# SiLU once instead of twice, its rounded part by a copy, and new orders around it, in a three-pass attention block

## The reference

```python
win = x cut into 8x8 windows                     # 16 windows of 64 tokens in an image
q, k, v = split(layernorm(win, ln1) @ in_w.T + in_b)          # 8 heads of 16
attn = softmax(q @ k.T / 4)                      # in a window
y = win + (attn @ v) @ out_w.T + out_b
h = layernorm(y, ln2)
y = y + silu(h @ fc1_w.T + fc1_b) @ fc2_w.T + fc2_b           # hidden width 256
# second layer, over the 1024 tokens of an image
q, k, v = wq @ y + bq, wk @ y + bk, wv @ y + bv               # width 64
out = wo @ ((q @ k.T / N) @ v) + bo + y
```

## Time and profile before

| | us |
|---|---|
| median of 3 runs | 342.38 (340.73 to 343.91) |
| the profiled execution, run time | 343.58 |
| its span in the profile | 341.8 |
| one even step (start of `b_score` to the next) | 17.39 |
| one odd step | 20.77 |
| epilogue, from its `b_score` to the end | 44.37 |

### The profile page before, as it was taken

How to read it: one execution, slowest core, us unless ns; L and a number is a source line. 1 busy time by engine, 2 the same in 40 slices (tenths; PEclk the granted TensorE clock), 3 DMA queues, 4 the chain that set the end, 5 groups by cost and what they waited for, 6 DMA issues and landing times. The chain is left out here.

```text
span 341.8 us, 9704 instructions
## 1 busy us (share of the span) xinstructions
PE 319.7 (94%) x3424; PEld 268.4 (79%) x3424; DVE 273.9 (80%) x851; ACT 238.4 (70%) x446; POOL 165.6 (48%) x177
## 2 busy tenths in 40 slices
PE   6789898999999999999999999999999999999675
PEld 5678787888787888778887888788887888787554
DVE  4776788988798969888798969898798879686752
ACT  5555486877869596967869595977878695955260
POOL 6514555538265544538265554537264653422430
PEclk9989899999999999999999999999999999999895
DMA  4442021221504032221404042222404041210011
GB/s 138 110 103 49 3 71 54 58 72 42 144 12 109 10 96 91 48 79 47 141 15 101 13 106 82 65 64 55 132 17 105 13 107 44 71 24 2 0 64 61
DMA packets 31888, 22.36 MB, mean 65 GB/s; under 512 B 22433, under 2 KB 23777, under 8 KB 31841
## 3 DMA queue, kind: packets, MB, share of 16 engines
q1 hardware_dynamic: 31744, 21.62, 23.3%
q10 hardware_dynamic: 96, 0.13, 0.1%
HBM read 4.95 MB, written 4.19 MB: 27 GB/s over the span
## 5 line engine op out<-in xcount | busy, mean ns | idle before, releaser
L1213 ACT ACTIVATE probs<-p_scoreT 128x512 f32<-128x512 f32 x64 | 37.8, 591 | 45.6 <-PE p_scoreT L781 44.8
L542 POOL TENSOR_TENSOR hid_l<-hid,hid_h 128x512 fp32r<-128x512 f32 x30 | 40.0, 1345 | 46.4 <-ACT hid_h L1248 40.4
L1504 DVE TENSOR_REDUCE row_max<-p_x 128x8 f32<-128x512 f32 x64 | 43.2, 683 | 7.7 <-PE p_x L749 7.7
L796 PEld LDWEIGHTS p_attn<-vd,probs 128*64 128x64 f32 x1024 | 36.2, 140 | 14.2 <-issue 9.5
L796 PE MATMUL p_attn<-vd,probs 128*64 128x34 f32 x1024 | 45.6, 245 | 1.1 <-DVE o_tok L1524 1.1
L777 PE MATMUL p_scoreT<-qd_h,kd_h 128*128 128x256 f32 x128 | 40.1, 313 | 2.6 <-issue 2.4
L513 POOL TENSOR_SCALAR x_res<-x_in,out_b 128x256 f32<-128x256 f32 x28 | 25.7, 927 | 29.0 <-issue 29.0
L526 POOL TENSOR_TENSOR rstd<-rstd,minus_half 128x4 f32<-128x4 f32 (+1 forms) x33 | 35.3, 1070 | 2.7
L777 PE MATMUL p_scoreT<-qd_l,kd_h 128*128 128x256 f32 x128 | 36.6, 286 | 0.0
L777 PE MATMUL p_scoreT<-qd_h,kd_l 128*128 128x256 f32 x128 | 36.6, 286 | 0.0
L524 POOL TENSOR_SCALAR rstd<-mv 128x4 f32<-128x4 f32 (+1 forms) x33 | 7.5, 228 | 56.9 <-DVE mv L1445 56.9
(11 more groups left out here) (249 smaller groups left out, 881.6 us busy)
## 6 DMA issues: line engine op xcount, KB each, us to landing
qd_l<-q_l SPq DMA_DIRECT2D x64, 64.0 KB, 2.0
vd<-v_tok SPq DMA_DIRECT2D x64, 64.0 KB, 2.2
qd_h<-q_h SPq DMA_DIRECT2D x62, 64.0 KB, 2.0
out<-out_sb SPq DMA_DIRECT2D x15, 256.0 KB, 2.6
x_in<-in_x SPq DMA_DIRECT2D x14, 256.0 KB, 2.9
x_first<-in_x SPq DMA_DIRECT2D x2, 256.0 KB, 2.7
fc_rows<-in_L_conv_fc_w SPq DMA_DIRECT2D x2, 128.0 KB, 2.6
out<-out_sb SPq DMA_DIRECT2D x2, 128.0 KB, 2.1
```

The costliest lines, as they stand in the source:

```text
L542: pool.tensor_tensor(hid_l[:, t], hid[:, t], hid_h[:, t].bitcast(F32), ALU.subtract).then_inc(hid_low[t], 1)
L796: last = pe.matmul(p_attn[64 * win:64 * win + 64, 2 * VB * j:2 * VB * (j + 1)], probs[:, p % 2, win, j, :], vd[:, h.par, 2 * p + win, :, : ...
L1213: act.activation(probs[:, p % 2], p_scoreT[:].rearrange("row (win j q) -> row win j q", win=2, j=QUADS), ACT.Exp, scale=SCORE_SCALE).then_ ...
L1504: dve.tensor_reduce(row_max[:, p].rearrange("row (j a) -> row j a", a=2), score(p).rearrange("row j (a k) -> row j a k", a=2), AXIS_X, ALU.max
```

## The change

ScalarE computes the SiLU once, into `hid`. DVE makes `hid_h` from it with a copy (`hidden_high`, 128 x 512, float32 to fp32r, both in SBUF), and GpSimd makes `hid_l` as before. This holds for halves 0 to 13, 28 copies in all; half 14 and the two parts of the last half keep both activations (`high_by_silu`). The copy of block 0 stands near the end of DVE's step, that of block 1 is the first instruction of DVE's next step; on GpSimd the subtraction of block 0 ends a step and that of block 1 opens the next. The two parts keep their hidden tiles in other buffers (`hidden_of`), so that they no longer wait for fc2 of half 14. All engines' orders of the second step, the even and the odd step and the epilogue are rearranged. At both ends: the load of half 3 is issued later by SP, `load_biases` comes before the last pair in the first step, and in front of three products at the end of the program stand 5, 5 and 8 products of a constant.

```diff
+        def hidden_of(h):
+            if h.early or h.late:
+                return qd_h[:, 0, 0:2], qd_h[:, 0, 2:4], x_in
+            return hid_h, hid_l, hid
+
+        def high_by_silu(h):
+            return h.early or h.late or 2 * h.loop.i + h.c == 2 * IMAGES - 2
...
             def even_step(loop, more):                       # GpSimd
-                residual(a)
+                hidden_low(tail, 1)
                 rstd2_of(c)
...
                 hidden_low(c, 0)
-                hidden_low(c, 1)
...
             def first_step(loop):                            # PE
                 b_attn(b, 2)
+                load_biases()
                 b_attn(b, 3)
-                load_biases()
...
             def even_step(loop, more):                       # PE
                 b_scoreT(b, 0)
+                c_project(c)
                 c_fc2(tail)
-                c_project(c)
...
                 c_fc1(c, 0)
+                c_fc1(c, 1)
                 b_attn(b, 3)
-                c_fc1(c, 1)
...
             def odd_step(loop):                              # PE
                 b_scoreT(b, 0)
+                c_fc2(tail)
                 c_project(c)
-                c_fc2(tail)
...
+                b_attn(b, 3)
+                d_final(loop, -1, 0, p_d)
                 c_fc1(c, 0)
-                d_final(loop, -1, 0, p_d)
                 c_fc1(c, 1)
                 d_final(loop, -1, 1, p_scoreT)
-                b_attn(b, 3)
...
             def epilogue(loop):                              # PE
+                c_kv(c)
                 c_kv(early)
                 c_kv(late)
+                d_final(loop, -1, 1, p_d)
+                d_kvT(loop, 0)
+                keep_clock(5, p_c[0])
                 d_bT(loop, 0)
+                keep_clock(5, p_c[0])
                 d_mT(loop, 0)
+                keep_clock(8, p_c[0])
                 d_final_last(loop)
...
             def c_silu(h, t):                                # ScalarE
-                act.activation(hid_h[:, t, h.cols], c_banks(h)[t][:, h.cols], ACT.Silu, ...).then_inc(hid_high[t], 1)
+                if high_by_silu(h):
+                    if not h.early and not h.late:
+                        act.wait_ge(fc2_ready, h.n(1))
+                    act.activation(hid_h[:, t, h.cols], c_banks(h)[t][:, h.cols], ACT.Silu, ...).then_inc(hid_high[t], 1)
                 act.activation(hid[:, t, h.cols], c_banks(h)[t][:, h.cols], ACT.Silu, ...).then_inc(hid_full[t], 1)
...
             def even_step(loop, more):                       # ScalarE
                 load_silu_table(b)
+                c_silu(c, 0)
                 a_v(a)
-                c_silu(c, 0)
                 c_silu(c, 1)
...
+            def hidden_high(h, t):                           # VectorE
+                dve.wait_ge(hid_full[t], h.n())
+                if h.follows(1):
+                    dve.wait_ge(fc2_ready, h.n(1))
+                dve.tensor_copy(hid_h[:, t], hid[:, t]).then_inc(hid_high[t], 1)
...
             def even_step(loop, more):                       # VectorE; the odd step and the epilogue begin alike
+                hidden_high(tail, 1)
                 b_max(b, 0)
                 b_widen(b, 0)
...
+                hidden_high(c, 0)
+                b_norm(b, 3)
...
             def epilogue(loop):                              # VectorE
-                d_mT(loop, -1)
                 c_y1(late)
                 c_stats(late)
                 c_aggregate(late)
-                c_norm(early)
...
+                c_norm(late)
+                d_mT(loop, -1)
                 c_yn(late)
```

More of the change, by code:

```diff
@@ L456, in step_even @@
                 spread_q(loop.half(1))
+                if not c:
+                    load_x(loop.half(3))
                 spread_v(loop.half(1))
@@ L598, in even_step @@
                     rstd1_of(next_a)
+                residual(a)
                 y2_low_part(tail)
@@ L722, in a_v @@
                 pe.wait_ge(xn_full, h.n())
-                if not h.second():
+                if h.follows(2):
                     pe.wait_ge(q_high, h.n())
@@ L849, in c_fc2 @@
                 pe.wait_ge(hid_low[1], h.n())
+                hid_h, hid_l, _ = hidden_of(h)
                 three_passes(c_banks(h)[1][:, h.cols], [weights(F2_), weights(F2_ + 1)],
@@ L1064, in epilogue @@
                 d_kvT(loop, -1)
+                c_project(early)
                 b_attn(b, 3)
                 c_back(c)
[L1067 removed]
+                c_yT(early)
+                c_transpose(late)
                 d_bT(loop, -1)
[L1069 removed]
+                c_project(late)
                 c_fc1(c, 0)
+                c_yT(late)
                 c_fc1(c, 1)
+                c_back(early)
                 d_mT(loop, -1)
[L1073 to L1079 removed]
                 c_back(late)
@@ L1599, in hidden_low @@
                 dve.wait_ge(hid_full[t], h.n())
-                dve.wait_ge(fc2_ready, h.n(1))
+                dve.wait_ge(hid_low[t], h.n(1))
+                hid_h, hid_l, hid = hidden_of(h)
                 dve.tensor_tensor(hid_l[:, t, h.cols], hid[:, t, h.cols], hid_h[:, t, h.cols].bitcast(F32), ALU.subtract
@@ L1699, in even_step, with odd_step @@
                 c_norm(c)
+                a_q(a)
+                c_kv(tail)
                 b_norm(b, 1)
-                a_q(a)
                 a_k(a)
                 c_yn(c)
-                c_kv(tail)
-                b_norm(b, 2)
                 if more:
                     a_norm(next_a)
+                b_norm(b, 2)
+                a_k_low_block(a)
+                hidden_high(c, 0)
+                b_norm(b, 3)
+            def odd_step(loop):
+                b, a, next_a, c, tail = loop.half(1), loop.half(2), loop.half(3), loop.half(0), loop.half(-1)
+                hidden_high(tail, 1)
+                b_max(b, 0)
+                b_widen(b, 0)
+                b_max(b, 2)
+                c_o(c)
+                b_max(b, 1)
+                b_max(b, 3)
+                c_y2(tail)
+                c_y1(c)
+                b_widen(b, 1)
+                a_xn(a)
+                c_kv(tail)
+                a_stats(next_a)
+                c_stats(c)
+                d_kvT(loop, -1)
+                b_norm(b, 0)
+                c_aggregate(c)
+                b_widen(b, 3)
+                a_aggregate(next_a)
+                a_q(a)
+                d_bT(loop, -1)
+                b_norm(b, 1)
+                c_norm(c)
+                a_k(a)
+                b_norm(b, 2)
+                d_mT(loop, -1)
+                c_yn(c)
+                a_norm(next_a)
```

193 lines of the change are left out of this document (76 added, 117 removed).

## The result

The changed kernel takes 350.33 us (median of 4 runs, 348.69 to 351.29), the kernel before 343.14 in the same comparison: a ratio of 1.0215 (95% interval 1.0143 to 1.0288). It is slower, by 1.4 to 2.9%. The profiled execution is the run of 348.69, with a span of 346.9 us, 5.1 more than before. The four runs took 348.69 and 349.55 us at a mean granted clock of 0.994 and 0.995, 351.11 and 351.29 at 0.985, while the profiled run of before (343.58, clock 0.974) lies above its median, so the two spans differ by less than the medians.

A forecast was written before the change was run, and what follows sets the result against it. The tensor engine bounds the kernel, busy for 94% of the span. Odd steps +4.5, even +2.1, epilogue -5, first steps -1 sum to +0.6 on 343.58: 344.2, or 343.0 us on the median's basis; range 332 to 353.

The forecast's parts named there:

- the likeliest case: Whole kernel: copy 1 gets ahead of subtraction 0 in even steps; 343.0 us, within 1%, chance 0.37.
- the slow rival: Even steps' opening: subtraction 0 starts ahead of copy 1, `c_project` starts at T+4.1; +11.2 us, time 352, chance 0.27.
- odd steps +4.5: Six odd steps' openings: held copies and `b_widen` make PE wait for `max_wide`; +0.75 us each, bounds +1.2 to +6.0.
- even steps +2.1: Seven even steps' openings: `c_project` ahead of fc2 makes PE need `o_l` first; +0.3 us each, bounds 0 to +3.1.
- epilogue -5: Epilogue: `y` wait and half clock go, constant products help, moved work costs +1.0; bounds -3 to -7.5 us.
- first steps -1: First steps: biases fill a 0.72 us hole, second and third steps have 0.88 + 0.97 idle; bounds 0 to -3.
- What a held copy costs: VectorE copies inside SBUF: stand still during a GpSimd subtraction, until about 0.15 us before its recorded end.
- the tie: End of odd steps: SiLUs 0.57 us apart against copy 0 plus hand-over to GpSimd, 0.43 + 0.14 = 0.57.
- ScalarE's saved 19 us: ScalarE: 28 activations of 0.69 us go; counted as nothing, since PE doesn't wait for ScalarE in dense steps.
- The 1.7 for the lower clock: Epilogue: PE's 3.40 us at clock 0.50 cost 1.7 us more than at full clock, and this can go.

The follow-up runs named there:

- The one-input operation above: Changed kernel with GpSimd's two-input subtraction replaced by a product of `hid` with zero, so fc2 gets no low part: 338.00 us, ratio 0.9847 to the kernel before.
- the added wait: Changed kernel with one wait more: GpSimd starts the subtraction of block 0 only after the copy of block 1 too; 344.10 us, ratio 1.0008 to the kernel before.
- the ends alone: Kernel before, its steps and activations kept, with the changed kernel's prologue, first step, epilogue, hidden tiles of the two parts and constant products: 337.29 us, ratio 0.9845.

## Why the prediction was partly right

The range held the time, but the likeliest case did not come. I forecast 343.0, no change; it is 350.3, close to the slow rival's 352. By the terms of the sum: odd steps +4.5 forecast and +2.8 measured, even steps +2.1 and +8.8, epilogue -5 and -4.75, first steps -1 and -1.72. The even steps make the difference.

- **What a held copy costs: right.** A copy waits until 0.15 us before GpSimd's recorded end: in the even opening 210.40 - 0.15 + 0.43 = 210.68, where copy 1 ended. The Trainium skill, *SBUF — State Buffer*, section "SBUF: two separate sides", has the same exclusive lock and a loser that fully blocks; the 14 openings agree but for those 0.15 us, for this two-input operation. The one-input operation above differs: it let copies run while it went on.
- **The odd step: mechanism right, size too large.** I had +0.75 and it is +0.49. `max_wide` came at 3.07 after the start where I had 3.43, since the chain of SiLU, copy and subtraction ran some 0.3 us earlier than I walked it. The hold alone is 0.92 (I had 1.0), and 0.43 comes back, more than the 0.25 that I allowed.
- **The even step: the step that failed is the tie.** I wrote that copy 1 gets ahead of subtraction 0 at 0.57 against 0.57. GpSimd won by 0.11 us: it started 0.09 behind copy 0, where I took 0.14 from the hand-over of ScalarE to GpSimd, and the second SiLU ended 0.6 behind the first. From there on it went as in the slow rival, with `c_project` at 3.93 for the 4.1 given there, +1.33 a step for its 1.6. With copy 1 ahead, by the added wait, the even step is 17.75 in three of five, and the forecast said 17.39 + 0.3 = 17.69. So the term for that case was good, and only the choice between the cases was wrong, at 0.37 against 0.27.
- **ScalarE's saved 19 us: right at nothing.** No kernel here that computes the SiLU once has a lower median than the ends alone, which compute it twice.
- **Epilogue: right, -4.75 for -5.** In detail less so: a new wait of 1.97 for `yn_tok`, which I didn't see, takes the place of the 2.77, and the constant products are worth 0.43 rather than 1.5. The 1.7 for the lower clock isn't shown either: in the run on the ends alone PE runs at 0.50 again for 3.41 us (from 317.34), and the epilogue is 39.70 all the same. That the sum came so near is in part luck.
- **First steps: -1.72 for -1 in the profile, but not shown to come from the change.** In the profile of before PE runs two stretches of 3.41 us at the clock of 0.50 in the first two steps (from 19.94 and 33.60), in the changed one a single stretch (from 31.83). The two runs on the ends, with and without the constant products, have the same beginning; they take 31.21 us for these steps at a mean clock of 1.00 (16.80 to 48.01) and 33.12 at 0.90 (17.98 to 51.10). So a difference of this size comes with the clock, where the kernels don't differ.

What stays open: the time rose by 7.2 us between the medians and by 5.1 between the two profiles. The difference goes with the granted clock of the runs, as said with the result. Why the clock falls in one run and not in another of the same kernel, no run here shows.

## What to carry to other kernels

When work is moved from one engine to another, look not only at the new engine's busy share (0.86 us fitted into 1.29 here) but at who runs beside each moved instruction, at the few places where the bounding engine has no slack. A race that comes out even on paper isn't a case to bet on: decide it with a wait in the order, and then walk the next instruction through the same meeting, because a hold that is taken off one copy can fall on the next. And try the parts of a change apart: here the ends alone win 1.5% and the rest of the change took 3.7% away.

## What was not expected of the hardware

What a VectorE copy inside SBUF suffers depends on GpSimd's kind of operation. A subtraction of two 128x512 tiles (1.28 us) held it until 0.15 us before the end. A product of one such tile with a constant (1.49 us) held it for the first 0.46 us and let it run from there to 0.99 at least; a one-input `kd_l` (1.57 us) held a VectorE operation that started 1.24 us after it. A copy written in a slower form (0.71 us for 0.43) was held until the same 0.15 us before the end, and where it started first, the subtraction took longer (1.50 to 1.57 us). And a two-input VectorE subtraction of 128x128 was held in the same way, 1.26 us for 0.29. `row_max`, which reads PSUM, took 0.69 though it began 0.27 us into such a subtraction, and 0.67 to 0.69 everywhere else in these two kernels.
